# A four-layer transformer kernel on one core: paired exponentials in layer 1, and a new table of places for all steps

## The reference

```python
q = _l2norm(q) * sm
k = _l2norm(k)
scores = jnp.einsum('bhqd,bhkd->bhqk', q, k)
probs = jax.nn.softmax(scores, axis=-1)
o = jnp.einsum('bhqk,bhkd->bhqd', probs, v)
```

## Time and profile before

| | |
|---|---|
| median of 3 runs | 1167.29 us (1166.8 to 1167.61) |
| the profiled execution | 1168.58 us |
| its span, first to last instruction | 1166.8 us |
| mean granted TensorE clock | 0.982 |
| PE, PEld busy | 1097.9 us (94%), 703.1 us (60%) |
| DVE, ACT, POOL busy | 706.4 us (61%), 807.1 us (69%), 491.8 us (42%) |

### The profile page before, as it was taken

How to read it: one execution, slowest core, us unless ns; L and a number is a source line. 1 busy time by engine, 2 the same in 40 slices (tenths; PEclk the granted TensorE clock), 3 DMA queues, 4 the chain that set the end, 5 groups by cost and what they waited for, 6 DMA issues and landing times.

```text
span 1166.8 us, 19882 instructions
## 1 busy us (share of the span) xinstructions
PE 1097.9 (94%) x6717; PEld 703.1 (60%) x6717; DVE 706.4 (61%) x1484; ACT 807.1 (69%) x1439; POOL 491.8 (42%) x447
## 2 busy tenths in 40 slices
PE   8799999889899999999999999999999999999985
PEld 6576877655664665656656657666656566545432
DVE  7454547535165265234775865865865865898874
ACT  3563655478787778897587686687687686676763
POOL 3452642523633625444334553354344344344232
PEclk9999999999999999999999999999999999999998
DMA  6000000313313203321122231122131121131301
GB/s 233 17 29 18 11 10 12 76 42 101 87 29 82 65 1 82 83 64 28 28 74 74 69 82 29 28 74 65 29 90 29 38 56 51 48 90 45 93 9 39
DMA packets 36387, 64.47 MB, mean 55 GB/s; under 512 B 7208, under 2 KB 22312, under 8 KB 36288
## 3 DMA queue, kind: packets, MB, share of 16 engines
q1 hardware_dynamic: 36288, 63.20, 20.4%
HBM read 22.90 MB, written 2.12 MB: 21 GB/s over the span
## 4 chain that ended last, share of the span: by engine, by line
PE 67%; ACT 11%; DVE 11%; issue 5%; POOL 4%; DMA 1%; ACTq 0%; SPq 0%; POOLq 0%; DVEq 0%
PE AVB L698 12%; PE ring L586 12%; PE ring L587 10%; PE ring L588 10%; PE ring L685 10%; PE ring L660 5%; ACT probs L876 4%; DVE m L1184 3%; PE ring L629 2%; ACT gT_h L942 2%; PE ring L718 1%; ACT gT_f L942 1%; ACT L876 1%; DVE stats L1042 1%; PE ring L723 1%
## 5 line engine op out<-in xcount | busy, mean ns | idle before, releaser
L876 ACT ACTIVATE probs<-ring 128x512 f32<-128x512 f32 x768 | 400.2, 618 | 125.8 <-PE ring L660 77.4
L1184 DVE TENSOR_REDUCE m<-ring 128x1 fp32r<-128x512 f32 x512 | 319.9, 682 | 109.8 <-PE ring L660 78.8
L685 PE MATMUL ring<-SQ,SK 64*128 64x512 f32 x768 | 238.9, 439 | 12.7 <-ACT probs L876 5.2
L660 PE MATMUL ring<-SK,SQ 63*128 63x512 f32 x512 | 197.8, 457 | 7.6 <-ACT probs L876 5.8
L685 PEld LDWEIGHTS ring<-SQ,SK 64*128 64x128 f32 x768 | 109.9, 185 | 146.8 <-issue 50.9
L698 PE MATMUL AVB<-probs,V 128*32 128x512 f32 x1536 | 195.3, 614 | 0.1
L1287 POOL TENSOR_TENSOR gT_l<-gT_f,gT_h 128x512 fp32r<-128x512 f32 x96 | 121.0, 1282 | 81.7 <-ACT gT_h L942 79.7
L586 PE MATMUL ring<-w_h,gT_h 128*128 128x256 f32 x384 | 110.4, 288 | 2.5 <-ACT gT_h L942 1.3
L660 PEld LDWEIGHTS ring<-SK,SQ 63*128 63x128 f32 x512 | 84.5, 184 | 39.5 <-ACT probs L876 31.2
L587 PE MATMUL ring<-w_l,gT_h 128*128 128x256 f32 x384 | 106.7, 278 | 0.0
L588 PE MATMUL ring<-w_h,gT_l 128*128 128x256 f32 x384 | 106.6, 278 | 0.0
(11 more groups left out here) (183 smaller groups left out, 2114.8 us busy)
## 6 DMA issues: line engine op xcount, KB each, us to landing
SQ<-qh SPq DMA_DIRECT2D x96, 128.0 KB, 2.6
SK<-kh SPq DMA_DIRECT2D x96, 128.0 KB, 2.8
SQ<-ql SPq DMA_DIRECT2D x48, 128.0 KB, 2.7
SK<-kl SPq DMA_DIRECT2D x48, 128.0 KB, 2.8
raw<-in_w SPq DMA_DIRECT2D x20, 256.0 KB, 2.8
wmod_s<-in_wmod SPq DMA_DIRECT2D x6, 512.0 KB, 3.9
gates<-gate_rows SPq DMA_DIRECT2D x12, 256.0 KB, 3.6
raw<-in_wqkv SPq DMA_DIRECT2D x9, 256.0 KB, 2.8
```

Of the source, the lines that this page charges most:

```text
L660: mm = pe.matmul(o[:, :], SQ[a % 4][r:r + KS, n // 2, c * P:(c + 1) * P], SK[a % 4][r:r + KS, n // 2, :], start=True, stop=True)
L685: mm = pe.matmul(o[:, :], SK[a % 4][r:r + KS + 1, n // 2, c * P:(c + 1) * P], SQ[a % 4][r:r + KS + 1, n // 2, :], start=True, stop=True)
L876: act.activation(probs[:, n % PROBS, :], bank(kind, a, i)[:, :], ACT.Exp, scale=SCALE[layer(unit_job(a))]).then_inc(done["scores"], 1)
L1184: nc.vector.tensor_reduce(m16[:, 80 * (a % 2) + col:80 * (a % 2) + col + 1], bank(kind, a, i)[:, :], AX_X, ALU.max, negate=True).then_inc( ...
```

## The change

Three things:

1. The 7 banks of the ring become one PSUM tensor `rings`, so that two neighbouring banks can be read as one.
2. For layer 1, where the scores of the two heads of a pair have consecutive uses and their banks are neighbours (`double`), one exponential reads both banks (128x1024) and writes two slots of `probs`; it waits for both products, and counts for two. Of the 128 pairs of layer 1 this is so for 103 (26, 28, 30 and 19 in jobs 4 to 7); 12 pairs have another ring step between them and 13 lie across the end of the ring. The step `max` gets the same code, but layer 1 has no such step, so it is never used there.
3. Nearly every table gets new values. The list has the same 2452 steps as before.

```diff
-        ring = [ctx.enter_context(nc.psum_tensor(f"ring{i}", [P, TOK], F32)) for i in range(RING)]
+        rings = ctx.enter_context(nc.psum_tensor("rings", [P, RING * TOK], F32))
+        ring = [rings[:, TOK * i:TOK * i + TOK] for i in range(RING)]
+
+        def double(kind, a, i):
+
+            first = USE[(kind, a, i - i % 2)]
+            return bounded(unit_job(a)) and USE[(kind, a, i - i % 2 + 1)] == first + 1 and first % RING < RING - 1
+
+        def two_banks(kind, a, i):
+            first = USE[(kind, a, i)] % RING
+            return rings[:, TOK * first:TOK * first + 2 * TOK].rearrange("p (n k) -> p n k", n=2)
...
-                elif kind == "scores":
-                    n = nth("scores", a, i) - 1
-                    act.wait_ge(pe_ring, use(kind, a, i))
+                elif kind == "scores" and not (double(kind, a, i) and i % 2):
+                    n, two = nth("scores", a, i) - 1, double(kind, a, i)
+                    act.wait_ge(pe_ring, use(kind, a, i + two))
...
-                    act.activation(probs[:, n % PROBS, :], bank(kind, a, i)[:, :], ACT.Exp,
-                                   scale=SCALE[layer(unit_job(a))]).then_inc(done["scores"], 1)
+                    if two:
+                        act.activation(probs[:, n % PROBS:n % PROBS + 2, :], two_banks(kind, a, i), ACT.Exp,
+                                       scale=SCALE[layer(unit_job(a))]).then_inc(done["scores"], 2)
+                    else:
+                        act.activation(probs[:, n % PROBS, :], bank(kind, a, i)[:, :], ACT.Exp,
+                                       scale=SCALE[layer(unit_job(a))]).then_inc(done["scores"], 1)
...
-START = [("stat1", 0, 0), ("load_mod", 0, 0), ("load_qkv", 0, 0), ("load_qkv", 0, 2), ("load_mod", 0, 1),
+START = [("load_w1", 0, 0), ("stat1", 0, 0), ("load_mod", 0, 0), ("load_qkv", 0, 0), ("load_qkv", 0, 2),
...
-PAIR_LAST = ("p10 A p6 0 p2 1", "p4 A p8 0 p4 1", "p6 a p6 0 p2 b p2 1", "p4 0 a p4 1 b", "p4 A p8 0 p4 1", "A p4 0 p4 1", "p8 a p8 0 p2 b p2 1", "p6 0 p2 a p4 1 p2 b")
+PAIR_LAST = ("p10 A p6 0 p2 1", "p4 A p8 0 p4 1", "p6 a p6 0 p4 b p2 1", "p6 0 a p4 1 b", "p6 A p8 0 p4 1", "A p6 0 p6 1", "p8 a p8 0 p2 b p2 1", "p6 A 0 p8 1")
```

More of the change, by code:

```diff
@@ L70 @@
            "norm2": (14.33,), "bias": (-5.4,)}
[L71 to L76, removed]
@@ L87 @@
[L87 to L90, removed]
+SINGLE2 = {"stat1": (-16.5,), "norm1": (-14.55,), "hT1": (-9.7, -9.49), "q": (-6.76, -3.06), "k": (-5.65, -3.6),
+           "v": (3.0, 4.07), "scores0": (-0.14, 0.81, 1.78, 4.23), "soft0": (2.59, 4.44, 5.01, 5.51),
+           "pT0": (7.92, 8.38, 8.63, 8.99), "av0": (12.74, 12.9), "proj": (13.98, 14.38), "stat2": (16.24,),
+           "norm2": (16.64,), "bias": (-0.3,)}
@@ L106 @@
[L106 to L113, removed]
-             "load_w2": (13.9, 16.35, 22.15, 22.75), "split_w2": (14.7, 17.6, 23.55, 25.05)}
@@ L126 @@
[L126 to L129 removed]
[3 rows of a table removed]
+FFN3 = {"hT2": (23.3, 23.76), "fc1": (25.6, 25.61, 25.72, 25.73, 29.65, 29.66, 29.67, 29.68), "gelu": (25.74, 29.69),
+        "fc2a": (26.65, 27.9), "fc2": (31.15, 31.55)}
@@ L135, in timed @@
+FFN1 = {"hT2": (17.27, 17.77), "fc1": (20.32, 21.68, 21.73, 21.79, 25.29, 25.65, 26.83, 28.08), "gelu": (22.14, 28.39),
+        "fc2a": (25.82, 27.37), "fc2": (34.2, 34.63)}
+START = [("load_w1", 0, 0), ("stat1", 0, 0), ("load_mod", 0, 0), ("load_qkv", 0, 0), ("load_qkv", 0, 2),
+         ("load_mod", 0, 1), ("load_qkv", 0, 1), ("load_w1", 0, 2), ("split_qkv", 0, 0), ("load_wp", 0, 0),
[3 rows of a table added]
 def timed(table, j):
@@ L1177, in _ @@
                                             ).then_inc(done[kind], 1)
-                elif kind == "max":
-                    n, c = i % 4, i // 4
-                    col = ((n % 2) * 2 + n // 2) * TT + c
-                    dve.wait_ge(pe_ring, use(kind, a, i))
+                elif kind == "max" and not (double(kind, a, i) and i % 2):
+                    n, c, two = i % 4, i // 4, double(kind, a, i)
+                    col = 80 * (a % 2) + ((n % 2) * 2 + n // 2) * TT + c
+                    dve.wait_ge(pe_ring, use(kind, a, i + two))
                     if i < 2 and a - 2 >= UNITS * BATCH:
                         dve.wait_ge(pe_ring, use("shift1", unit_job(a - 2), 1) if bounded(unit_job(a - 2)) else use("shift", a - 2, 1))
-                    nc.vector.tensor_reduce(m16[:, 80 * (a % 2) + col:80 * (a % 2) + col + 1], bank(kind, a, i)[:, :], AX_X, ALU.max,
-                                            negate=True).then_inc(done["max"], 1)
+                    if two:
+                        nc.vector.tensor_reduce(m16[:, col:col + 9:8], two_banks(kind, a, i), AX_X, ALU.max,
+                                                negate=True).then_inc(done["max"], 2)
+                    else:
+                        nc.vector.tensor_reduce(m16[:, col:col + 1], bank(kind, a, i)[:, :], AX_X, ALU.max,
+                                                negate=True).then_inc(done["max"], 1)
                 elif kind == "shift":
```

73 lines of the change are left out of this document (42 added, 31 removed), and 12 rows, old and new, of tables (FIRST, START).

## The result

| | before | after |
|---|---|---|
| median of 6 runs | 1167.7 us (1166.8 to 1170.87) | 1163.49 us (1162.21 to 1166.24) |
| the profiled execution | 1168.58 us | 1162.71 us |
| its span, mean granted clock | 1166.8 us, 0.982 | 1160.9 us, 0.983 |

The ratio is 0.9963, with a 95% interval of 0.9951 to 0.9975: 4.3 us faster, where 3.6 were forecast. That agreement flatters the working. Most of the gain comes from one string of places in job 7, which the forecast met only as a share of "one fall of the clock", and the operation that gives the change its name adds nothing that can be measured.

What follows compares the result with a forecast made beforehand. TensorE was taken to bound the kernel, with ScalarE pacing about a sixth of layer 1. Terms -1.1 + 0 + 1.0 - 0.2 - 1.1 - 0.5 - 1.7 = -3.6 us gave a 1163.7 us median; 8-in-10 range 1154 to 1170.

Steps and rivals of the forecast that it cites:

- one fall of the clock: Layer 1: one of six falls from 2.4 to 1.2 GHz was expected to go, 1.7 us less, bounds 0 and 10.
- The paired exponential: Layer 1: one exponential over two banks replaces two single ones, 1.1 us less, ends nothing and 4.0 us.
- 22 pairs on the chain: Layer 1: 26 us of exponentials on the chain were counted as 22 doubled pairs, each saving 0.05 us.
- Banks held longer: Layer 1: a pair gives its first bank back 0.44 us later and the second 0.05 earlier; priced at 0.
- a rival at 0.13: Layer 1: pairs hold banks too long, costing 5.5 to 11 us; 1171 us with half the waits, chance 0.13.
- The start: Before layer 0's first products: the earlier `load_w1` and moved weight split each delay by 0.5 us, 1.0 us more.
- Layer 0: `fc2a` placed ahead of projections that wait 0.22 us for GpSimd's `hT_l`: 0.2 us less.
- Layer 3, the cast: Jobs 12 to 14: the cast of `cT` no longer follows the normalisation; job 14's waits go, 1.1 us less.
- The end: Eight products with V come ahead of the last two scores, removing a 0.48 us wait: 0.5 us less.
- Layers 2 and 3 otherwise: Moved steps hidden beside a nearly full TensorE: taken as 0, with 2 us either way.
- The likeliest case: Whole kernel: the forecast itself, 1163.7 us for the median, own range 1160.5 to 1166, chance 0.45.
- the rival in which all falls go: Layer 1: every clock fall and the wait before it goes, 8.5 us less for falls, 1155 us; chance 0.22.

Runs made afterwards that it cites:

- the pairs alone: The kernel before with the 103 doubled exponentials added and all its old tables kept: 1167.66 us, ratio 1.0002 to the kernel before.
- the tables only: The change with the doubling switched off, so every exponential is single and all steps keep their new places: 1163.7 us, ratio 0.9963 to the kernel before.

## Why the prediction was right, and where it was not

- **The paired exponential (-1.1 forecast): none measured.** The duration was right: 1037 ns for an estimate of 1056. Four doubles in a row take 3.76 us in the change's trace (first row below), that is 0.907 us from start to start where two single ones take 0.97, so a pair saves 0.063 us, not 0.05. The Trainium skill (ScalarE: Activation LUTs, What ACT_TABLE_LOAD costs) gives 186 ns + 0.833 ns per column, by which I estimate 1039 ns here, and the row agrees; the saving of 93 ns per pair that follows from its overlap does not. The step that failed is "22 pairs on the chain": it took a share of the chain for time that goes when the exponential is shorter. At 401 us, the wait that the prediction named, GpSimd took the place at once, and the banks held longer take some of it back.

```profile
238.65 3.76 ACT L888 ACTIVATE probs<-rings 128x1024 f32<-128x1024 f32 x4
...
260.00:265.00 5.00, 3.95 (x22) 2.18 (x22) 2.62 (x6) 5.00 (x9) 0.00 (x0) 1.00 0.01 3
```

- **Banks held longer (0 forecast, and a rival at 0.13).** The mechanism exists: score products wait twice as long (6.3 against 3.2 us). It did not cost the 5.5 to 11 us of the rival: with and without the pairs the ratio is 0.9963, and the pairs alone have 1.002 at most, 2.3 us. The two should have been one term.
- **The clock (-1.7 for one fall of six).** Right in kind and size, in part by luck. The fall at 525 us is gone for good and explains about 1.7 us of TensorE's busy time; but 0.6 us more of busy time went with it, and 1.2 us of waits, which the sum had priced at nothing. The reason given ("if waits for ScalarE shorten and the steps around them are retimed") holds here through the order of products and not through the pairs. The fall that the prediction pointed at was another, at 402 us, behind the wait of 2.01 us. Neither trace of the change has it, but the other twelve do, the tables only (0.66 from 400 to 405 us) and the pairs only (0.76) among them, and the wait never shortened, so it is not borne out. Other falls come and go: that at 260 us is gone in the second row above, but the same trace has new ones at 240 and 270 us.
- **The start (+1.0).** Its sign is likely by two couples of kernels (1.4 and 1.8 parts in a thousand, with overlapping intervals); of its two halves the split is 0.33 us by the rows, and the issue is not told from scatter. The second `hT_l` came at 15.85 us and not at 16.4. Nine traces with the old list have it at 15.25 in the mean and five with the new one at 15.76: 0.5 us later, half of the term.
- **Layer 0 (-0.2).** Not seen, and too small to be. All of layer 0's tables together are 1.0000, to 1.6 us either way.
- **Layer 3, the cast (-1.1).** The two waits of 0.22 and 0.85 us are gone, as forecast, but "nothing is lost" was wrong. Job 14's normalisation runs beside the scores of job 15, after what the table calls the end of job 14. TensorE at the shift before, then TensorE and VectorE after the change:

```profile
1121.16 0.31 PE L677 MATMUL ring<-unit,m 64*16 64x64 f32 x2 [0.94 <-DVE m L1184]
```

```profile
1115.29 0.31 PE L688 MATMUL rings<-unit,m 64*16 64x64 f32 x2 [1.67 <-DVE m L1203]
...
1116.26 0.33 DVE L1210 CAST cT<-rings 16x64 fp32r<-16x64 f32 x2
1116.52 1.36 DVE L1102 TENSOR_SCALAR tok<-X,mv,rstd 128x256 f32<-128x256 f32 x4
```

The product with V that now fills the time of cast and DMA no longer fills that of the maxima, where TensorE waits 1.67 us instead of 0.94. Of 1.07 us, 0.73 went back. All seven traces with the new tables of layer 3 wait 1.66 or 1.67 us here, and all seven with the old ones 0.92 to 0.94. That is the cover I had named and priced at nothing. And in job 14, which holds the same move for job 13's rows, the new tables lose 0.8 us.

- **The end (-0.5).** The wait of 0.48 us is gone and sixteen products stay behind the last score instead of 32. From that shift to the end of job 15 are 28.4 us against 28.8, for this and the cast together: 0.4 of the 1.6 forecast.
- **Layers 2 and 3 otherwise (0, with 2 either way).** By my own test the forecast was to be called wrong beyond 2 us, and jobs 8 to 12 gave 0.9 + 1.9 = 2.8. Of the part in job 12, 1.1 us is idle time of TensorE and 0.9 busy time, which the row of one batch in layer 2 could not show; I had read no stretch of layer 3 but its end. Some of it is spent again in job 14.

The sum of what the traces show is -3.4 in job 7, -0.9, -1.9, and 0 to +1 after, with nothing from layers 0 and 1 before job 7: -5 to -6, against -4.3 by the medians, which the scatter of single traces covers. The likeliest case was the right one of the four, and the rival in which all falls go is out: five falls remain in layer 1. That the total fits is luck in good part: the pairs, the cast and the end fell short by 2.3 us together, and jobs 7 to 12 gave 4.5 us more than the one term for them, the 1.7 of the clock.

## What to carry to other kernels

A faster instruction on an engine that is waited for is worth its saving only where nothing it holds (here a bank) is given back later, and where no other engine ends the same wait; price the bank with the saving, and look up every producer of a wait, not only the one that the profile names. Where an engine must leave its stream for a long stretch, here GELU between two table loads, feed it before that and give the array work that needs nothing from it: one reordering of scores and products with V did more than 103 faster exponentials. Cut several traces at fixed instructions and read only the columns that do not scatter; a lead at the first milestone was gone 440 us later.
